# A sorted edge list on one core: the row of `dst` that holds a boundary is picked by a matmul instead of an indirect DMA, and the load of `x` is split

## The reference

```python
def _mp_layer(x, src, dst, edge_attr, W, b):
    loops = arange(n); src2, dst2 = [src, loops], [dst, loops]; ea2 = [edge_attr, 0]
    msg = concatenate([x[dst2], x[src2], ea2], axis=1) @ W + b
    return relu(segment_sum(msg, dst2, num_segments=n))
h   = relu(_mp_layer(x, src, dst, edge_weight1, W1, b1))      # 64 -> 128
out = _mp_layer(h, src, dst, edge_weight1, W2, b2)            # 128 -> 64
return layernorm(x + log_softmax(out, axis=1))
```

## Time and profile before

| | |
|---|---|
| median of three runs | 251.34 us (251.25, 251.34, 252.3) |
| span of the profiled execution, first to last instruction | 251.8 us |
| its own time | not listed apart; of the three times only the 252.3 is longer than this span |
| mean granted PE clock | 0.972 of full |
| PE busy / PEld / DVE / ACT / POOL | 202.7 / 183.9 / 180.2 / 115.1 / 165.0 us |

### The profile page before, as it was taken

One profiled execution on the slowest core, in us unless ns is written; L12 is line 12 of the kernel. 1 busy time (PEld: TensorE's weight loads), 2 busy tenths in 40 slices (PEclk: granted clock), 3 DMA queues, 4 the chain that ended last, 5 costly groups with the idle time before them and its releaser, 6 DMA issues.

```text
span 251.8 us, 5544 instructions
## 1 busy us (share of the span) xinstructions
PE 202.7 (81%) x2089; PEld 183.9 (73%) x2089; DVE 180.2 (72%) x436; ACT 115.1 (46%) x235; POOL 165.0 (66%) x338
## 2 busy tenths in 40 slices
PE   1001269599998999989999899989999999999940
PEld 0000159489887898879888798878888999999930
DVE  4035999979876899768977789768410285899881
ACT  2020173267766676757766776667741010101110
POOL 5728998619999999999999999999846000000000
PEclk9999999779999999999999999999999999999995
DMA  1543200000000000000000000000000001010000
GB/s 35 136 115 85 63 21 21 0 3 1 3 2 3 0 3 3 1 3 1 3 1 3 0 3 0 4 0 5 0 3 0 3 3 31 3 31 23 19 15 18
DMA packets 12578, 4.18 MB, mean 17 GB/s; under 512 B 11911, under 2 KB 12126, under 8 KB 12551
## 3 DMA queue, kind: packets, MB, share of 16 engines
q1 hardware_dynamic: 10711, 1.77, 4.0%
q0 software_dynamic: 1840, 2.04, 3.0%
HBM read 2.98 MB, written 0.81 MB: 15 GB/s over the span
## 4 chain that ended last, share of the span: by engine, by line
PE 42%; POOL 34%; DVE 12%; DMA 5%; issue 4%; ACT 1%; POOLq 0%; ACTq 0%; DVEq 0%
PE pset L834 21%; PE acc L826 9%; PE pset L801 5%; POOL u L378 4%; POOL deg L377 4%; DMA adj<-in_dst,adj 4%; POOL t L390 3%; DVE ohl L504 3%; POOL t L394 3%; POOL z L389 3%; POOL u L381 3%; POOL zr L392 3%; POOL base L400 2%; POOL z L398 2%; POOL z L396 2%
## 5 line engine op out<-in xcount | busy, mean ns | idle before, releaser
L715 ACT ACTIVATE adj<-pset 125x1000 bf16<-125x1000 f32 x75 | 77.3, 1032 | 7.0 <-PE pset L801 7.0
L826 PE MATMUL acc<-x,adj 125*125 125x195 bf16 x625 | 75.7, 260 | 2.2 <-POOL x L329 2.2
L504 DVE TENSOR_TENSOR ohl<-iota,keyl 128x1000 bf16<-128x1000 bf16 (+1 forms) x75 | 60.0, 800 | 12.6 <-PE dense L814 11.8
L801 PE MATMUL pset<-ohr,ohl 128*125 128x125 bf16 x600 | 60.0, 255 | 6.0 <-DVE ohr L504 6.0
L826 PEld LDWEIGHTS acc<-x,adj 125*125 125x125 bf16 x625 | 59.7, 143 | 5.7 <-POOL x L329 2.4
L504 DVE TENSOR_TENSOR ohr<-iota,keyr 128x1000 bf16<-128x1000 bf16 (+1 forms) x75 | 60.7, 810 | 0.0
L801 PEld LDWEIGHTS pset<-ohr,ohl 128*125 128x125 bf16 x600 | 50.8, 154 | 7.9 <-DVE ohr L504 6.3
L834 PE MATMUL pset<-z,adj 125*125 125x192 bf16 x625 | 52.8, 247 | 0.0
L834 PEld LDWEIGHTS pset<-z,adj 125*125 125x125 bf16 x625 | 51.7, 136 | 0.3
L529 DVE TENSOR_REDUCE s_sum<-acc 125x65 f32<-125x195 f32 x25 | 9.1, 363 | 19.1 <-PE acc L826 18.7
L751 ACT ACTIVATE x<-x 125x192 f32<-125x192 f32 (+2 forms) x6 | 2.6, 427 | 38.5 <-DVE x L586 38.5
(11 more groups left out here) (114 smaller groups left out, 271.0 us busy)
## 6 DMA issues: line engine op xcount, KB each, us to landing
x_nat<-in_x SPq DMA_DIRECT2D x1, 781.2 KB
out<-x SPq DMA_DIRECT2D x2, 187.5 KB
out<-x SPq DMA_DIRECT2D x3, 93.8 KB
out<-x SPq DMA_DIRECT2D x1, 125.0 KB
adj<-in_dst,adj POOLq DMA_INDIRECT x5, 7.1
adj<-in_edges,adj POOLq DMA_INDIRECT x5, 4.0
adj<-in_edge_attr,adj POOLq DMA_INDIRECT x5, 3.5
se_scratch<-adj SPq DMA_DIRECT2D x5, 2.4 KB
```

The lines of the kernel that those rows point to most:

```text
L504: ins = dve.tensor_tensor(out=oh[s][:, :, :, :], in0=iota2[:, 0:Q, :].unsqueeze(1).broadcast_to([128, n, Q, 2]), in1=key[:, g, k0:k0 + 2 * ...
L715: act.activation(adj4[0:Q, g, :, w0:w0 + 8 * WD].rearrange("p h (b e) -> p b h e", b=2), pset[s][0:Q, :, 0:4 * WD * G].rearrange("p b (h e ...
L801: ins = pe.matmul(pset[s][0:Q, i // 4, 0:4 * WD * G].rearrange("p (h e) -> p h e", h=G)[:, :, i % 4 * WD:(i % 4 + 1) * WD], ohl[s][:, i // ...
L826: ins = pe.matmul(acc[0:Q, 0:XW], adj4[0:Q, g, h, :], x3[:, h, :], start=(h == 0), stop=(h == G - 1))
```

## The change

`dst` is loaded whole: the array that the host lays out has two more columns (the first value of the row, -1 for row 0, and the first value of the next row, N for the last), and one DMA on SP brings all 125 rows (427 integers each) into `dst_rows`. Which row holds a window's first edge is a comparison of the window's threshold with these two values; DVE writes it as a one-hot `pick` (row by window) with two instructions per block, and PE multiplies `pick` with the rows as fp32 (`rows_f`, 425 values and, as column 426, the index of the row's first edge). The picked rows stand in PSUM, where DVE counts as before. The x load is in two DMAs: groups 0 to 7 right behind `dst_rows`, groups 8 to 24 after SP has waited for the pairs of block 0 (`pairs_in[0]`). ACT and POOL wait for both.

```diff
+            gp.iota(iota5, [[WD, Q]], ...).then_inc(pick_consts, 1)
+            gp.iota(block_of, [[Q * WD, J]], ...).then_inc(pick_consts, 1)
+            gp.iota(rows_f[:, EC:EC + 1], [[0, 1]], base=0, channel_multiplier=EC, ...).then_inc(pick_consts, 1)
...
-            for j in range(4):
-                gather_rows(j)
             gather_edges(0)
-            gather_rows(4)
             gather_attrs(0)
...
+            dve.wait_ge(dst_in, 16)
+            dve.tensor_copy(rows_f[:, 0:EC], dst_rows[:, 2:EC + 2]).then_inc(rowsf_ready, 1)
+            dve.wait_ge(pick_consts, 3)
+            dve.tensor_tensor(edge_of, dst_rows[:, 0:2]..., block_of..., ALU.subtract).then_inc(pickch, 1)
+            def pick_row(j):
+                dve.tensor_scalar(past[:, j, :], iota5, edge_of[:, j, 1:2], None, ALU.is_gt).then_inc(pickch, 1)
+                dve.wait_ge(pickch, j + 2)
+                dve.scalar_tensor_tensor(out=pick[:, j, :], in0=iota5, scalar=edge_of[:, j, 0:1],
+                                         in1=past[:, j, :], op0=ALU.is_gt, op1=ALU.subtract).then_inc(pick_ready, 1)
+            def row_bank(j):
+                return pset[j // 2][0:Q, j % 2, :]
             def offset(j):
-                dve.wait_ge(rows_in[j], 16)
-                link(dve.scalar_tensor_tensor(out=junk[:, j, :], in0=rows[:, j, :], scalar=thr[:, j:j + 1],
+                dve.wait_ge(rows_done, j + 1)
+                link(dve.scalar_tensor_tensor(out=junk[:, j, :], in0=row_bank(j)[:, 0:EC], scalar=thr[:, j:j + 1],
...
-            pe.matmul(acc[0:Q, 0:Q], samp_b, ident[0:Q, 0:Q], start=True, stop=True).then_inc(sampm_ready, 1)
+            pe.wait_ge(rowsf_ready, 1)
+            pe.wait_ge(pick_consts, 3)
+            for j in range(J):
+                pe.wait_ge(pick_ready, j + 1)
+                pe.matmul(pset[j // 2][0:Q, j % 2, 0:EC + 1], pick[:, j, :], rows_f, start=True, stop=True)\
+                  .then_inc(rows_done, 1)
...
-                sp.dma_start(samp, dst[:, 0:1]).then_inc(samp_in, 16)
-            sp.dma_start(x_nat[:, :, :], x.rearrange("(g q) c -> q g c", q=Q)).then_inc(xnat_in, 16)
+            sp.dma_start(dst_rows, dst).then_inc(dst_in, 16)
+            xg = x.rearrange("(g q) c -> q g c", q=Q)
+            sp.dma_start(x_nat[:, 0:XA, :], xg[:, 0:XA, :]).then_inc(xnat_in, 16)
+            sp.wait_ge(pairs_in[0], 16)
+            sp.dma_start(x_nat[:, XA:G, :], xg[:, XA:G, :]).then_inc(xnat_in, 16)
```

More of the change, by code:

```diff
@@ L41 @@
 KW = 26
+XA = 8
 KB = 12
@@ L106, in gnn @@
         x_rest = tail([Q, G, C], FP32)
-        samp = tail([Q, 1], I32)
+        dst_rows = tail([Q, EC + 2], I32)
+        rows_f = tail([Q, EC + 1], FP32)
+        edge_of = tail([Q, J, 2], FP32)
+        block_of = tail([Q, J], FP32)
+        iota5 = tail([Q, Q], FP32)
+        past = tail([Q, J, Q], FP32)
+        pick = tail([Q, J, Q], FP32)
         ones = tail([Q, EC], BF16)
@@ L223, in gnn @@
             "base_ready", "z_stored", "fin", "fin_act", "out_stored")}
-        samp_in = sem("samp_in")
+        dst_in = sem("dst_in")
         w_in = sem("w_in")
@@ L229, in gnn @@
         xnat_in = sem("xnat_in")
-        rows_in = [sem(f"rows_in{j}") for j in range(J)]
         pairs_in = [sem(f"pairs_in{j}") for j in range(J)]
@@ L237, in gnn @@
         consts = sem("consts")
-        sampb_ready = sem("sampb_ready")
-        sampm_ready = sem("sampm_ready")
-        rowidx_ready = sem("rowidx_ready")
+        pick_consts = sem("pick_consts")
+        rowsf_ready = sem("rowsf_ready")
+        pick_ready = sem("pick_ready")
+        rows_done = sem("rows_done")
+        pickch = sem("pick_chain")
         off_ready = sem("off_ready")
@@ L282, in _ @@
         def _(gp):
+            gp.iota(iota5, [[WD, Q]], base=0, channel_multiplier=0,
+                    allow_small_or_imprecise_dtypes=True).then_inc(pick_consts, 1)
+            gp.iota(block_of, [[Q * WD, J]], base=0, channel_multiplier=0,
+                    allow_small_or_imprecise_dtypes=True).then_inc(pick_consts, 1)
+            gp.iota(rows_f[:, EC:EC + 1], [[0, 1]], base=0, channel_multiplier=EC,
+                    allow_small_or_imprecise_dtypes=True).then_inc(pick_consts, 1)
+            gp.iota(thr[:, :], [[Q * WD, J]], base=0, channel_multiplier=WD,
+                    allow_small_or_imprecise_dtypes=True).then_inc(pick_consts, 1)
+            gp.memset(ones[:, :], 1.0).then_inc(pick_consts, 1)
             gp.memset(ident[:, :], 0.0).then_inc(consts, 1)
-            gp.iota(thr[:, :], [[Q * WD, J]], base=0, channel_multiplier=WD,
-                    allow_small_or_imprecise_dtypes=True).then_inc(consts, 1)
-            gp.wait_ge(consts, 2)
+            gp.wait_ge(consts, 1)
             gp.affine_select(out=ident[:, :], in_=ident[:, :], compare_op=ALU.not_equal, fill=1.0,
                              base=0, pattern=[[-1, 128]], channel_multiplier=1).then_inc(consts, 1)
-            gp.memset(ones[:, :], 1.0).then_inc(consts, 1)
-            gp.wait_ge(consts, 4)
+            gp.wait_ge(consts, 2)
             gp.tensor_copy(ident16[:, :], ident[:, 0:Q]).then_inc(consts, 1)
@@ L299, in _ @@
             gp.memset(x3[:, :, 2 * XC + C:3 * XC], 0.0).then_inc(consts, 1)
[L300 to L304, removed]
             def gather_edges(j):
@@ L331, in _ @@
                 gather_attrs(j)
-            gp.wait_ge(xnat_in, 16)
+            gp.wait_ge(xnat_in, 32)
             def split_sums(j):
@@ L440, in link @@
                 dve.wait_ge(dch, chain[0])
-            dve.wait_ge(samp_in, 16)
-            dve.tensor_copy(samp_b, samp.broadcast_to([Q, Q])).then_inc(sampb_ready, 1)
-            dve.wait_ge(consts, 3)
+            dve.wait_ge(dst_in, 16)
+            dve.tensor_copy(rows_f[:, 0:EC], dst_rows[:, 2:EC + 2]).then_inc(rowsf_ready, 1)
+            dve.wait_ge(pick_consts, 3)
+            dve.tensor_tensor(edge_of, dst_rows[:, 0:2].unsqueeze(1).broadcast_to([Q, J, 2]),
+                              block_of.unsqueeze(2).broadcast_to([Q, J, 2]), ALU.subtract).then_inc(pickch, 1)
@@ new lines, in _ @@
+            dve.wait_ge(pickch, 1)
+            def pick_row(j):
[5 more added lines that the diff above has]
+                return pset[j // 2][0:Q, j % 2, :]
@@ new lines, in offset @@
+            def offset(j):
+                dve.wait_ge(rows_done, j + 1)
+                link(dve.scalar_tensor_tensor(out=junk[:, j, :], in0=row_bank(j)[:, 0:EC], scalar=thr[:, j:j + 1],
+                                              in1=ones[:, :], op0=ALU.is_lt, op1=ALU.mult,
+                                              accum_out=cnt2[:, j:j + 1]))
+                dve.scalar_tensor_tensor(out=off_idx[:, j:j + 1], in0=row_bank(j)[:, EC:EC + 1], scalar=1.0,
+                                         in1=cnt2[:, j:j + 1], op0=ALU.mult, op1=ALU.add).then_inc(off_ready, 1)
@@ L446, in _ @@
+            pick_row(0)
+            pick_row(1)
+            dve.wait_ge(pick_consts, 5)
+            offset(0)
+            for j in range(2, J):
+                pick_row(j)
+            dve.wait_ge(consts, 2)
             dve.tensor_reduce(bmask[:, :], ident[0:KB, 0:KB].rearrange("p (a b) -> p b a", b=3), AX.X, ALU.add)\
                .then_inc(bchain, 1)
[L448 to L453, removed]
@@ L466, in _ @@
-            for j in range(J - 1):
+            for j in range(1, J):
                 offset(j)
@@ L512, in _ @@
             keys(0, 1)
-            offset(J - 1)
-            dve.wait_ge(consts, 11)
+            dve.wait_ge(consts, 9)
             dve.wait_ge(keys_ready, 1)
@@ L1018 @@
     edges = _np.concatenate([edges, _np.full((128, 2), N, edges.dtype)], axis=0)
-    dst_rows = _np.asarray(dst).reshape(Q, -1)
+    first = _np.asarray(dst)[::E // Q][1:]
+    dst_rows = _np.concatenate([_np.concatenate([[-1], first])[:, None], _np.concatenate([first, [N]])[:, None],
+                                _np.asarray(dst).reshape(Q, -1)], axis=1).astype(_np.int32)
     attr = _np.concatenate([_np.asarray(edge_weight1)[:, 0], _np.zeros(128, _np.float32)])[:, None]
```

19 lines of the change are left out of this document (2 added, 17 removed).

## The result

The changed kernel takes 252.76 us (median of 20 runs, 251.52 to 254.95) against 251.64 us of the kernel before (20 runs, 250.67 to 252.61): a ratio of 1.0041 with a 95% interval of 1.0023 to 1.0059. It is a little slower, 1.1 us; 249.8 was forecast, with 252.6 as the upper end of the range.

The account below looks back on a forecast made before the run. Bound: the prologue chain to the end of keys(1, J) on DVE. x at 21.9, one-hots from 24.2, plus 2.9 + 3.5 + 14.1 gives 44.7 against 46.25: 1.5 us won, 249.8 us on the median, range 246.3 to 252.6.

Parts of the forecast that it names:

- It ran 0.4 above the median of 251.34: Base: the profiled span of 251.8 us taken as that execution's time; 1.5 us won gave 249.8 on the median.
- the price of the row gathers and a slow start: x load before, 5.5 us late: some 1.9 at the start, 3.6 where it met row gathers of 850 KB.
- The arrival of x: Second part of x, asked for at 13.4, there at 21.9 (18.7 to 25), 5.1 us later than before.
- a sign of being wrong: ACT's cast waiting past 23.4 for x; the change was to gain only while x arrives before that.
- the 2.2 that I had worked out and set aside: Cost of edge gathers 1 to 4 (512 KB) to x's second part: 2.2 us by ratio, 0 at best, 1.2 taken.
- the prediction's formula: The end of keys(1, J) on DVE is the arrival of x plus 22.9 us.
- the rival with x as bound: x's second part, asked for at 13.4, arrives at 24.0: 251.9 us, or 252.7 with the matmul's upper end; chance 0.15.
- the search for the first edges: Prologue from dst_rows through pick and fp32 matmul (1.8 us): gather at 9.1, pairs at 13.4, 8.0 us sooner than before.
- the first collision: DVE one-hots standing beside POOL's first subtraction: 2.9 us lost instead of 3.6; beside the second, 3.5 as before.
- swallowing behind the keys: Rival: layer1 of group 0, POOL's work or PE's clock gives the gain back before the loop, 251.3 us; chance 0.18.
- The term that I set to nothing: PE granted 0.50 of its clock at 47 to 50 us; up to 1.3 us won if it falls otherwise.
- The fit of the Trainium skill: 2.0 us plus bytes over 436 GB/s: x at 16.7, 6.7 us won, 244.6 us; as a rival, chance 0.03.

Follow-up runs that it names:

- 33 runs of before: Further unedited executions of the kernel before, taken beside the experiments; only one has a span as long as 251.8 us (252.1), the others 248.9 to 250.6.
- the execution first read: The profiled execution of the unedited kernel before that the prediction was made from: span 251.8 us, keys(1, J) ending at about 46.25.
- with the gathers out of its way: Changed kernel with POOL's edge gathers 1 and 2 behind its first subtraction, 3 and 4 behind its second, weights 1 to 4 last: 256.5 us, ratio 1.0201.
- the run with the keys first: Changed kernel with ACT's first copy_keys ahead of its cast of x: 248.12 us, ratio 0.9865.
- the two new ones: The kernel before profiled twice more, no edit: times 251.05 and 251.81 us, spans 249.1 and 249.9.
- with 8 of 25 groups: Kernel before with only the x load split, 8 groups first and 17 after SP waits for the pairs of block 0: 257.24 us, ratio 1.0227.

## Why the prediction was wrong

- **The base it was taken from.** The failing step is "It ran 0.4 above the median of 251.34", and with it 46.25 as the end of the keys before. The execution that I read was late by 1.4 to 1.5 us at that point; two others end at 44.7 and 44.8. A sign stood there: I took the span for the time. With the 1.9 to 2.0 us that lie outside the span in 33 runs of before, 251.8 belongs to some 253.7, above each of the 20 times of before (of the 33 one was longer, 254.09). Where the lateness came from is shown only as far as the DMAs: a load of x that began slowly and arrived at 16.76 instead of 12.0, and a row gather 1.4 to 1.6 us longer. I had explained x's 5.5 us of delay as the price of the row gathers and a slow start; in the other executions it arrives at 11.9 to 12.1, nearly the 11.3 of its own rate.
- **The arrival of x**, the second term that failed, forecast 21.9, measured 23.52. This is past 23.4, which the prediction had named as a sign of being wrong. Three terms: the pairs at 13.9 instead of 13.4; the part by itself 7.9 us instead of 7.3; the gathers 1.7 instead of 1.2, nearer to the 2.2 that I had worked out and set aside. The sum is 1.6.
- **How the miss adds up.** A gain of 1.5 us was forecast and a loss of 1.1 measured. Of these 2.6 us, 1.5 are the base and 1.4 the end of the keys in the changed kernel (46.08 instead of 44.7: 1.6 from x, less 0.3 behind it, and rounding); some 0.3 went the other way behind the keys, mostly the shorter end. Both terms failed by about the same, and either alone would have all but eaten up the forecast gain.
- **The range was too narrow for its own terms.** Its upper end was 252.6. By the prediction's formula, x at its own upper bound of 25 gives keys at 47.9 and some 253.0, and the rival with x as bound had 252.7 as its longer price. The measured 252.76 lies between them.
- **Right:** the search for the first edges. `dst` brought DVE to its cast at 5.09, the fp32 matmul took 1.77 us (1.8 forecast, in bounds of 0.89 to 2.56), the gather is issued at 9.46 (9.1), `keys(0, 1)` ends before x and waits for it.
- **Right:** from the arrival of x to the end of the keys 22.9 forecast, 22.56 measured; the first collision costs less than before (3.34 us for one instruction, not 4.29), the second the same.
- **Right in part:** no swallowing behind the keys. From the reduction of group 1 to that of group 24 the changed kernel keeps the distance of before, 132.2 us. The term that I set to nothing, the clock behind the keys for "up to 1.3 us", is real and was well sized: 5.84 to 7.10 us between two reductions in three executions of before. That the clock fell in the changed kernel as in the execution first read (0.54 in both) was luck, as nothing in the prediction could tell it.
- **The rival that came true** is "the second part of x is the new bound", which had 0.15 (x at 24.0, 251.9). It stood against an end of the keys that was itself 1.4 us too late; with 44.8 the gain would have had to come from an arrival before 22.2, and the forecast of 21.9 would have been hardly a gain at all. The fit of the Trainium skill ("DMA: Bandwidth & Descriptors", "Anatomy of one DMA"), which is for transfers issued from GpSimd, gave x at 16.7, 6.8 us too early for this load from SP; 83 GB/s were measured for this part with the gathers out of its way.

## What to carry to other kernels

A load that is made to wait for another has to be followed to whoever needs its last byte, through the order of the engine that takes it in: here ACT's cast of x stood ahead of a copy that didn't need x, and a wait that freed one gather by about 1 us cost 7.5. Before a difference is taken from a profile, check that its execution is a usual one: the time minus the span is nearly constant here (1.9 to 2.0 us before, 1.8 to 1.9 in the changed kernel), and an arrival that is far later than the load's own rate may be that execution's alone. And a median of one kernel can hide executions 1 us apart: compare those of like clock. Elementwise work given to POOL wasn't free here while DVE worked at the same time: two operations of 3.14 us on POOL cost DVE 6 to 7 us, where DVE does them itself in 1.8 each.

## What the runs showed of the hardware

- DVE stood beside POOL's `tensor_tensor` also in fp32 work with one input and a constant: L493 took 3.91 us over 512 columns in the run with the keys first, and 0.43 in the changed kernel. The Trainium skill ("GPSIMD Engine Reference", "Specifications") says that the SBUF interfaces are shared, with contention for DVE instructions with two inputs or in a two-port mode. The one-hots have two inputs and agree with that; that L493 runs in such a mode is not shown by any row.
- DVE's cast of `dst` was not held by the long iota, which had ended: an iota of 125 fp32 columns took 0.24 us, not the 0.75 that 6.0 ns a column from the bf16 one of 256 gave.
- PE's granted clock in 46 to 53 us differed between executions of the same kernel (0.76 and 0.67 in the two new ones, 0.54 in the one first read), and with it the time from one reduction to the next (5.84, 6.73 and 7.10 us).
- An x load beside it slows the first indirect row gather: 7.4 to 8.95 us with all of x in flight, 5.24 with 8 of 25 groups.
